# Weighing rounds that run on over tile borders in a four-head attention: 86 for 96, sums in five or six pieces, output rows copied in two parts

## The reference

```
Q = (nx @ Wq.T), 4 heads of 32            # nx: 2048 normalised rows
Kc = nx @ Wkc.T; Vc = nx @ Wvc.T          # one key and one value of 32 values per row, shared by the heads
attn = softmax(Q @ Kc.T / sqrt(32))       # 4 heads x 2048 x 2048
O = attn @ Vc;  X = X + O @ Wo.T
```

## Time and profile before

| | |
|---|---|
| median of 3 runs | 675.39 us (674.88 to 676.74) |
| the profiled execution | 676.3 us, span 674.2 us |
| PE busy | 606.9 us, 90% of the span |
| DVE, ACT, POOL busy | 484.5, 352.5, 355.1 us |
| mean granted PE clock | 0.967 of full speed |
| chain that ended last | PE 71%, DVE 15%, ACT 5% |
| four-head attention | 318.3 to 580.6 us of the span |

### The profile page before, as it was taken

One profiled execution on the slowest core, in us unless ns is written; L12 is line 12 of the kernel. 1 busy time (PEld: TensorE's weight loads), 2 busy tenths in 40 slices (PEclk: granted clock), 3 DMA queues, 4 the chain that ended last, 5 costly groups with the idle time before them and its releaser, 6 DMA issues.

```text
span 674.2 us, 12623 instructions
## 1 busy us (share of the span) xinstructions
PE 606.9 (90%) x4528; PEld 407.2 (60%) x4529; DVE 484.5 (72%) x1140; ACT 352.5 (52%) x714; POOL 355.1 (53%) x369
## 2 busy tenths in 40 slices
PE   4876799967998889896999999999999999999996
PEld 2554699845774556554555555455555553688885
DVE  5763344424985778769877778888888883788986
ACT  2642455323665455452576766676676666533231
POOL 6507300073553545170678887888787868624311
PEclk9998999978997899998999999999999998999999
DMA  9701012210000000000000000000000000000101
GB/s 294 317 3 54 23 49 62 62 48 16 1 1 1 1 2 3 2 2 2 0 1 1 1 0 2 1 1 1 0 1 1 1 0 1 1 1 1 32 1 32
DMA packets 16616, 17.33 MB, mean 26 GB/s; under 512 B 1712, under 2 KB 15024, under 8 KB 16176
## 3 DMA queue, kind: packets, MB, share of 16 engines
q1 hardware_dynamic: 15536, 14.49, 6.4%
q0 software_dynamic: 1024, 2.10, 1.0%
HBM read 11.34 MB, written 5.24 MB: 25 GB/s over the span
## 4 chain that ended last, share of the span: by engine, by line
PE 71%; DVE 15%; ACT 5%; issue 4%; another core or an unknown queue 3%; DMA 1%; POOL 1%; SPq 0%; DVEq 0%; ACTq 0%
PE ps L2049 13%; PE ps L2039 10%; PE ps L2029 8%; PE ps L2177 5%; PE ps L1764 4%; PE ps L1853 3%; DVE region L1086 3%; PE ps L1747 2%; PE ps L2167 2%; PE ps L2169 2%; PE ps L2168 2%; PE ps L1843 2%; PE ps L1942 2%; ACT region L1372 1%
## 5 line engine op out<-in xcount | busy, mean ns | idle before, releaser
L1086 DVE TENSOR_REDUCE region<-ps 128x1 f32<-128x512 f32 x256 | 160.8, 684 | 38.6 <-PE ps L2029 38.1
L1537 ACT ACTIVATE region<-ps 128x512 f32<-128x512 f32 x256 | 138.1, 600 | 58.8 <-PE ps L2039 58.7
L767 POOL TENSOR_TENSOR region<-region 128x512 f32<-128x512 f32 x80 | 109.0, 1365 | 42.4 <-ACT region L1537 38.6
L2039 PE MATMUL ps<-qmr,kr 98*128 98x512 f32 x256 | 111.8, 441 | 2.6 <-ACT region L1537 1.8
L2029 PE MATMUL ps<-kr,qmr 96*128 96x512 f32 x256 | 102.8, 411 | 2.0 <-DVE region L1086 1.2
L2049 PE MATMUL ps<-region 128*32 128x512 f32 x512 | 93.1, 608 | 0.0
L2056 PE MATMUL ps<-region,ones 128*32 128x512 f32 x192 | 92.9, 606 | 0.2 <-DVE region L1103 0.2
L772 POOL TENSOR_TENSOR region<-region 128x512 f32<-128x512 f32 x64 | 82.0, 1282 | 11.8 <-ACT region L1537 8.0
L2039 PEld LDWEIGHTS ps<-qmr,kr 98*128 98x128 f32 x256 | 48.7, 191 | 54.2 <-issue 28.4
L2029 PEld LDWEIGHTS ps<-kr,qmr 96*128 96x128 f32 x256 | 49.0, 193 | 15.8 <-DVE region L1086 9.1
L1764 PE MATMUL ps<-region 128*128 128x128 f32 x272 | 40.6, 297 | 18.9 <-ACT region L1384 15.7
(11 more groups left out here) (283 smaller groups left out, 1206.6 us busy)
## 6 DMA issues: line engine op xcount, KB each, us to landing
region<-in_w SPq DMA_DIRECT2D x2, 2048.0 KB, 13.0
slots_in<-zeros SPq DMA_DIRECT2D x1, 1536.0 KB, 9.0
region<-slots_in SPq DMA_DIRECT2D x6, 256.0 KB, 2.8
slots_out<-og SPq DMA_DIRECT2D x6, 256.0 KB, 2.4
e<-in_e SPq DMA_DIRECT2D x1, 1152.0 KB, 15.7
x<-in_x SPq DMA_DIRECT2D x4, 256.0 KB, 4.0
out<-y SPq DMA_DIRECT2D x3, 256.0 KB, 2.3
e<-in_e SPq DMA_DIRECT2D x1, 576.0 KB, 16.6
```

Source lines behind the costliest of these rows:

```text
L767: ins = pool.tensor_tensor(o, held(tiles[0]), held(tiles[1]), ALU.add)
L1086: dve.tensor_reduce(mxp[:, u // HM, u % HM:u % HM + 1], bank(b), AX.X, ALU.max).then_inc(mx_read, 1)
L1537: act.activation(pm[:, t // 2, t % 2 * HM * P:(t % 2 + 1) * HM * P], bank(SCORE_BANKS[n % 3]), ACT.Exp, scale=SCM).then_inc(p_whole, 1)
L2039: pe.matmul(bank(SCORE_BANKS[n % 3]), kr[0:M_ROWS, t * P:(t + 1) * P], qr[0:M_ROWS, parity, :], start=True, stop=True).then_inc(st_filled, 1)
```

## The change

The rounds are cut from one list of all 256 (tile, step) pairs, three at a time, so that a round may hold the last steps of one tile and the first of the next: 85 rounds of three and one of one, 86 in all. The slots repeat every 48 steps. Each round has one sum product still, which belongs to the tile of the round's first step. A tile whose number divides by three begins six rounds and has the six pieces of before; every other tile begins five, and has five pieces of 4, 3, 3, 3 and 3 steps: POOL makes 3 + 2 + 2 + 2 additions for the first four and the first of the last piece's two, 10 in all, and DVE adds step 15. The sums move from the last group of bank 6 to the first. Where a round holds steps of two tiles, the rows of the groups that already belong to the new tile are copied out ahead of it (`sums_begun`, ahead of exponent 2), and the rest afterwards (`sums`, now ahead of exponent 6 instead of 4).

```diff
-ROUNDS = [(0, 1, 2), (3, 4, 5), (6, 7, 8), (9, 10, 11), (12, 13, 14), (15,)]
-PIECES = [(0, 1), (2, 3, 4), (5, 6, 7), (8, 9, 10), (11, 12, 13), (14, 15)]
-ROUND_SLOT = (8, 8, 14, 14, 19, 19)
+ROUNDS = [[(n // NT, n % NT) for n in range(k, min(k + PARTS, NT * NT))] for k in range(0, NT * NT, PARTS)]
+ROUND_SLOTS = (8, 8, 14, 14, 17, 20, 26, 26, 32, 32, 35, 42, 42, 48, 48, 51)
+PIECES = {6: [(0, 1), (2, 3, 4), (5, 6, 7), (8, 9, 10), (11, 12, 13), (14, 15)],
+          5: [(0, 1, 2, 3), (4, 5, 6), (7, 8, 9), (10, 11, 12), (13, 14, 15)]}
-SUM_PAIR = 2
+SUM_PAIR = 3
+SUM_EARLY = 1
...
+def rest_of(i):
+    keys = ROUNDS[round_of(i, NT - 1)]
+    return DM * (1 + sum(j == i for j, _ in keys)) if keys[-1][0] != i else P
...
+                last = p == len(pieces_of_tile(i)) - 1
+                here = tiles[1:-1] if last else tiles[1:]
+                if q >= SUM_RING:
+                    pool.wait_ge(round_done, round_of_piece(q - SUM_RING) + 1)
+                for n, t in enumerate(here):
+                    pool.wait_ge(p_whole, i * NT + t + 1)
+                    if n == 0:
+                        ins = pool.tensor_tensor(o, held(tiles[0]), held(t), ALU.add)
+                    else:
+                        pool.wait_ge(sum_step, adds_until(i, p, n))
+                        ins = pool.tensor_tensor(o, o, held(t), ALU.add)
...
                 dve.wait_ge(p_whole, i * NT + NT)
+                if len(tiles) == 2:
+                    dve.wait_ge(round_done, round_of_piece(q - SUM_RING) + 1)
+                    ins = dve.tensor_tensor(o, held(tiles[0]), held(tiles[1]), ALU.add)
+                else:
+                    dve.wait_ge(sum_step, adds_until(i + 1, 0, 0))
+                    ins = dve.tensor_tensor(o, o, held(tiles[-1]), ALU.add)
+                ins.then_inc(last_sum_ready, 1)
...
+            def sums_begun(i):
+                if rest_of(i) == P:
+                    return
+                act.wait_ge(round_done, round_of(i, NT - 1))
+                act.wait_ge(o_turned, i)
+                act.activation(oT[rest_of(i):P, :], bank(6)[rest_of(i):P, :], ACT.Copy).then_inc(oT_begun, 1)
...
-                act.activation(oT[:, :], bank(6), ACT.Copy).then_inc(oT_ready, 1)
+                act.activation(oT[0:rest_of(i), :], bank(6)[0:rest_of(i), :], ACT.Copy).then_inc(oT_ready, 1)
...
+                    if n > i and keys[g - 1][0] == i:
+                        pe.wait_ge(oT_begun, sum(rest_of(j) < P for j in range(n)))
...
+                    for k in range(len(ROUNDS)):
+                        if slot_of_round(k) == i * NT + t:
+                            weigh(k)
```

More of the change, by code:

```diff
@@ L152, in maxima_at, with slot_of_round, round_of, summed_in @@
     return [(i + 2, t - MAX_START) if t >= MAX_START else (i + 1, t + NT - MAX_START)]
[L155 to L167, removed]
+def slot_of_round(k):
+    return k // len(ROUND_SLOTS) * PARTS * NT + ROUND_SLOTS[k % len(ROUND_SLOTS)]
+def round_of(i, t):
+    return (i * NT + t) // PARTS
+def summed_in(i):
+    return [k for k, keys in enumerate(ROUNDS) if keys[0][0] == i]
+def pieces_of_tile(i):
+    return PIECES[len(summed_in(i))]
+def pieces_until(i):
+    return sum(len(pieces_of_tile(n)) for n in range(i))
+def piece_of(i, t):
+    return [p for p, tiles in enumerate(pieces_of_tile(i)) if t in tiles][0]
+def round_of_piece(q):
+    return [k for i in range(NT) for k in summed_in(i)][q]
+def adds_until(i, p, n):
+    pieces = [tiles for j in range(i) for tiles in pieces_of_tile(j)[:-1]] + pieces_of_tile(i)[:p]
+    last = [pieces_of_tile(j)[-1] for j in range(i)]
+    return sum(len(tiles) - 2 for tiles in pieces) + sum(len(tiles) - 2 for tiles in last) + n
+def rest_of(i):
+    keys = ROUNDS[round_of(i, NT - 1)]
+    return DM * (1 + sum(j == i for j, _ in keys)) if keys[-1][0] != i else P
 def cuts(sizes):
@@ L781, in shared_tile @@
             def shared_tile(i, parity, first=False, more=True):
-                for p in range(POOL_PIECES):
-                    whole_sum(i, p, first)
+                for p in range(len(pieces_of_tile(i))):
+                    whole_sum(i, p)
                 if 0 <= i - HALVES_TILE < ES:
@@ L1599, in shared_tile @@
                 for k in range(PAIRS):
+                    if k == SUM_EARLY and not first:
+                        sums_begun(i - 1)
                     if k == SUM_PAIR and not first:
@@ L2145, in shared_tile @@
                         prepared[stage](g)
[L2146 to L2150 removed]
+                    for k in range(len(ROUNDS)):
+                        if slot_of_round(k) == i * NT + t:
+                            weigh(k)
             over_tiles(shared_tile)
[L2153 to L2155 removed]
+            for k in range(len(ROUNDS)):
+                if slot_of_round(k) >= NT * NT:
+                    weigh(k)
             def hidden(j, e):
```

79 lines of the change are left out of this document (35 added, 44 removed).

## The result

The changed kernel takes 682.2 us (median of 13 runs, 677.2 to 684.9) beside 675.4 us before (13 runs, 672.9 to 679.2): 1.008 of the time before, 95% interval 1.0058 to 1.0102. That ratio on 675.4 is +5.4 us (3.9 to 6.9); the same kernel once more in another set of runs gave 1.0053 (1.0029 to 1.0076), +3.6.

What follows compares the result with a forecast made beforehand. PE was taken as the bound. -7.3 - 1.0 + 7.0 + 3.6 + 0.6 = +2.9 us; 676.3 + 2.9 - 0.9 = 678.3 us, range 669.5 to 685.5; the forecast alone (chance 0.45) within 675.5 and 682.

Steps and rivals of the forecast that it cites:

- Fewer rounds: PE, four-head attention: 33 pairs and 20 single rounds replace 48 pairs, -7.3 us, bounds 0 and 9.3.
- A wait that goes: Tiles 5, 7, 9, 11, 13: the pair at step 3 no longer waits for step 0's exponent, 5 x 0.2, -1.0 us.
- The last sum: Single round at step 3: PE waits for DVE's addition, locked out by POOL's, +7.0 us, bounds 1.5 and 8.1.
- The rival by which DVE goes first: DVE's last sum starts ahead of POOL's addition: +1.5 for +7.0, 672.8 us; chance 0.2.
- the one by which PE stays without any: PE stays without gaps, the waits filled or shorter, so the whole -8.3 arrives: 667.1 us; chance 0.15.
- Rounds moved to step 10: Score product of step 9 waits for exponent 6 behind two ACT copies, 0.4 in nine tiles, +3.6 us, bounds 0 and 5.
- DVE behind: After a late last sum DVE's maxima lag by 0.1 to 0.15 in four tiles, +0.6 us.
- The copy in two parts: Ten more ACT copies of 0.50 ahead of exponent 2, covered by ACT's idle time: 0; uncovered, at most 5 us.
- Sums in five pieces: POOL makes 10 additions for 9 in ten tiles, covered: 0, with 0.2 us of room at step 10.
- The rival by which POOL becomes the bound: Second round at step 10 waits for POOL's additions, 0.8 in each of ten tiles: +8 on the forecast, 686; chance 0.2.
- The end of the stage: Tiles 14 and 15, with POOL's inverse root one addition later: nothing beyond what the count of rounds already holds.
- The check by PE's idle time: Sign that the forecast is right: PE's idle time in the attention stage grows by some 11 us.

Runs made afterwards that it cites:

- ACT order: Changed kernel with ACT's sums copy ahead of exponent 4 or 5 and its query copy behind exponent 6: 1.005 of the kernel before.
- copy twice: Changed kernel with ACT's early copy of output rows made twice in its ten tiles: 1.0081 of the kernel before.
- the dose: Changed kernel with POOL's first addition made twice in the ten tiles of five pieces: 1.0131 of the kernel before.
- sum first: Changed kernel with DVE's last sum behind the maximum of step 0 instead of step 1: 0.9955 of the kernel before.
- splits early: Changed kernel with DVE's last sum, query low half and division earlier, ACT's sums and query copies reordered, early output copy moved: 0.9903 of the kernel before.

## Why the prediction was right

The direction and the mechanism came out; the size is short. 682.2 us lies in the range of 669.5 to 685.5, but 0.2 above the band that the forecast had by itself, and the forecast said 678.3. By its own terms, for tiles 1 to 13, where the profile says +4.1 (tile 0 took the same, tiles 14 and 15 +2.0; by the ratios the whole is +3.6 and +5.4):

- *Fewer rounds*, -7.3 in the stage: a pair measured 1.85 and a single round 1.00 (0.98 was taken, from the earlier trace rows), each with the same 0.19 beside it. In tiles 1 to 13 that is 25 pairs and 18 singles for 39 pairs: 51.0 + 21.4 for 79.6, -7.2; at the prediction's 2.05 and 1.17 these counts come to -7.6. The term holds to 0.4.
- *A wait that goes*, -1.0: in tiles 5, 7, 9, 11 and 13 the round that follows after three steps starts 1.59 to 1.61 after the resume, as unhindered steps would bring it, with nothing of the 0.2 left. It holds.
- *The last sum*, +7.0 (6.4 of it in these tiles): 7.9 measured, and 0.6 in tile 14. The sizes are those worked out, 1.53 in tiles 5 and 9 and 0.63 to 0.65 in 2, 3, 6 and 12; wrong were tile 8 (0 was taken, 0.74 measured, POOL 0.02 ahead) and tile 11 (1.0 taken, 1.53 measured). This is the term that was mis-sized, by 1.5. Its mechanism is shown from both sides: parting the two additions took 6.4 and 4.5 us off tiles 1 to 13. The Trainium skill ("SBUF — State Buffer", Who interferes with whom) says that two such instructions shut each other out and that the order of issue decides who waits; by that rule every tile pays in which POOL is ahead, and the trace agrees: 1.72 to 1.81 us in all nine. It doesn't go for every POOL instruction that reads SBUF: beside POOL's powers DVE's additions keep their 0.68 (the rows are under the last heading), and there the measurement decides. At the margin the start in the trace isn't the order either: in tile 8 of the changed kernel's second profile DVE starts 0.01 ahead of POOL (454.45 for 454.46) and still takes 1.84. The rival by which DVE goes first is out, and with these gaps the one by which PE stays without any.
- *Rounds moved to step 10*, +3.6, with *DVE behind*, +0.6: the gaps ahead of these nine pairs are 6.4 us over unhindered steps (0.51 in tiles 1 and 4, 0.52 in 13, 0.57 to 0.94 in the others). Of this 2.0 was there before at other places: 0.09 to 0.12 ahead of step 8 in tiles 5, 7, 9, 11 and 13, 0.71 in tile 10, and 0.37, 0.35 and 0.09 ahead of step 14 (and the resume behind it) in tiles 7, 10 and 11. That leaves 4.4 for 4.2. The sum was right and its cause was in part another: ACT's order is the cause in tiles 1, 4, 7 and 10 (0.5 each, gone with ACT order), but in 2, 5, 8 and 11 DVE's maxima are late as well, by the last sum and by the division that POOL locks out for 1.1 us behind it, and ACT's order alone changed 0 to 0.35 us there. The prediction had seen no collision of the division. So the late sum is paid twice, at step 3 and again at step 10, and that 4.4 came out beside 4.2 is in part luck.
- *The copy in two parts*, 0: copy twice shows it for the kernel as it is; once the last sum is early, 0.3 us of the copy come to light in tiles 5 and 11. *Sums in five pieces*, 0 with 0.2 us of room: the dose shows the 0; the room was 0.8 to 1.0 in tiles 1, 2 and 4, 0.3 in 13 and none in 8. The rival by which POOL becomes the bound is out.

-7.2 - 1.0 + 7.9 + 4.4 = +4.1, what tiles 1 to 13 show; foretold were -7.6 - 1.0 + 6.4 + 4.2 = +2.0. What the forecast is short by in these tiles is the last sum above all.

*The end of the stage* was taken to come to the count of rounds (+0.3), with 0.6 for the last sum in tile 14. In the profiles it is +2.0, with POOL's inverse roots one addition later and ACT waiting 1.40 us for them. But the changed kernel's clock is at 1.2 GHz for 6.8 us of it and that of the kernel before for 3.4, and by the estimate above (1.9 us for 6.8) some 1.0 of the +2.0 is the clock's; that the rest costs this much over many executions isn't shown.

The check by PE's idle time ("grows by some 11 us") was a bad one: by the groups of score, maximum, weighing and sum products it grew from 0.9 to 3.3 in tiles 1 to 13, since a wait begins under products that still count as busy.

## What to carry to other kernels

Where work is packed closer, list what each piece still needs at its new place and how many us after the last resume that is ready; here 8.3 us less of PE's work and waits were eaten by one operand that came 0.6 to 1.5 us late in nine tiles, and by what it, a second collision behind it and the order of ACT's copies held up six steps later. Two such lags aren't priced apart: an engine that comes late out of the first takes the cover from the second. And where a VectorE addition and a GpSimd addition meet within 0.1 us of each other, move the one that the busiest engine waits for by a step: that one line turned 1.008 (1.0058 to 1.0102) into 0.9955 (0.9934 to 0.9976), each beside the kernel before in its own set of runs.

## What the runs showed of the hardware

- A DVE addition (two inputs in SBUF) that starts behind a POOL addition ends 0.55 to 0.56 us after that one's end: in all nine tiles of the changed kernel (407.49 for 406.94 in tile 5; 458.17 for 457.62 in tile 8, where POOL was only 0.02 ahead), in the kernel before (548.83 for 548.27), and behind the split of an expert's weights of 0.72 (380.82 for 380.26 in sum first). Alone it takes 0.68, so no more than 0.13 of it lies beside the other. The division of 0.28 behaves alike: it ends 0.15 after POOL's addition.
- POOL's powers (two inputs in SBUF as well, L634 and L833) don't hold it so. These are the changed kernel's rows of the first power of the router and of the last DVE addition, 0.32 behind it:

```profile
587.13 5.44 POOL L833 TENSOR_TENSOR region<-region 128x32 f32<-128x32 f32 x1
...
587.45 0.68 DVE L1145 TENSOR_TENSOR region<-region 128x512 f32<-128x512 f32 x1
```

In sum first, tile 7, the inverse root (L634, 1.04 us from 413.05) is 0.42 ahead of the DVE addition, which takes 0.68 as well. The other way round it does wait: in tile 11 DVE is 0.10 ahead, and the inverse root takes 1.48 for 1.04.
- Two single rounds cost PE 0.34 us more than a pair (2 x 1.00 + 0.19 for 1.85). In a pair the four sets of four products (413.46 to 414.77 in tile 5 of the changed kernel) start 0.43 to 0.45 apart, and the score product follows 0.54 behind the last; a single round has one such step of 0.45 and then 0.55.
- Executions of one kernel in one set of runs differ with the granted clock: the kernel before took 672.4 us at a mean of 0.972 and 679.7 at 0.963, and splits early 667.7 at 0.970 and 676.1 at 0.951. In tile 15, behind the place where PE stood idle for 1.1 to 1.8 us, TensorE's clock fell to 1.2 GHz for 3.4, 6.8 or 13.7 us in twelve of the fourteen profiles and stayed at 2.4 GHz in two, and not the same in two profiles of one kernel (6.8 us at a stretch, and twice 3.4). These are the stretches in the kernel before and in the changed one:

```profile
567.70:571.00 3.30, 3.30 (x17) 0.83 (x17) 0.00 (x0) 1.94 (x4) 3.22 (x3) 0.50 0.00 0
```

```profile
573.70:580.40 6.70, 6.70 (x25) 2.74 (x26) 0.00 (x0) 3.99 (x8) 5.08 (x4) 0.50 0.00 0
```

In the changed kernel's a pair of rounds takes 3.57 us for 1.85. A gain below 2 us in such a stretch can't be read from one profile.
